# Another merge of all step chains in a two-layer kernel, with K's parts, the first stack transfers and heads 0 and 1's maxima written ahead of the second batch's FFN tail

## The reference

```
x = x + L0_ffn( L0_cond(cond, x) )          # gated FFN with quantised activations and ternary weights, inner 512
x = x + L1_ffn( L1_cond(x, cond) )
# L1_cond: 16-head causal attention (head size 8) with one extra "image" key and value per batch
# L1_ffn:  16-head full attention, layer norm, 8 experts chosen by a two-level router, layer norm
```

## Time and profile before

| | |
|---|---|
| median of 3 runs | 344.09 us (341.87 to 345.22) |
| profiled execution | 342.62 us, its span 340.5 us |
| PE busy | 286.8 us (84%) |
| DVE busy | 252.2 us (74%) |
| ACT busy | 178.2 us (52%) |
| POOL busy | 54.7 us (16%) |
| chain that ended last | PE 54%, DVE 22%, issue 16%, ACT 5%, DMA 1% |

### The profile page before, as it was taken

The page is one execution under the profiler, slowest core; times in us unless marked ns, Lnnn a source line. Parts: engine busy times, 40 slices in busy tenths (PEclk is TensorE's granted clock), DMA queues, the critical chain, the costliest instruction groups (busy, mean ns, idle before and its releaser), DMA issues.

```text
span 340.5 us, 5253 instructions
## 1 busy us (share of the span) xinstructions
PE 286.8 (84%) x1760; PEld 140.5 (41%) x1760; DVE 252.2 (74%) x754; ACT 178.2 (52%) x262; POOL 54.7 (16%) x121
## 2 busy tenths in 40 slices
PE   0363754888899999889899999999999999999992
PEld 0241432243343443433333332334344447777671
DVE  6978660999988769999999898888742133758646
ACT  2755449007575776475378866755668831221120
POOL 3069300001342332233300000002000000101001
PEclk9999995569999999999999999999999999999998
DMA  6893324711535004660014450070000000000101
GB/s 179 197 189 72 58 69 140 170 30 50 167 71 121 1 4 135 146 134 2 3 42 139 95 141 0 4 247 0 2 2 2 0 1 2 1 2 0 33 0 31
DMA packets 14990, 22.82 MB, mean 67 GB/s; under 512 B 2222, under 2 KB 12338, under 8 KB 14196
## 3 DMA queue, kind: packets, MB, share of 16 engines
q1 hardware_dynamic: 14676, 22.21, 25.4%
q0 software_dynamic: 288, 0.28, 0.6%
HBM read 13.99 MB, written 4.72 MB: 55 GB/s over the span
## 4 chain that ended last, share of the span: by engine, by line
PE 54%; DVE 22%; issue 16%; ACT 5%; DMA 1%; POOLq 0%; POOL 0%; SPq 0%; DVEq 0%; ACTq 0%
PE ps_pv L1391 13%; PE ps_t L1371 10%; PE ps_s L1348 10%; DVE mx L1066 8%; PE ps_s L1466 4%; PE ps_misc L1479 4%; DVE shared L1062 3%; DVE mx L1062 1%; DMA X<-in_x 1%; ACT probs L755 1%; DVE probs L995 1%; PE ps_misc L1324 1%; PE ps_misc L1328 1%; PE ps_misc L1354 1%; PE ps_t L1281 1%
## 5 line engine op out<-in xcount | busy, mean ns | idle before, releaser
L824 ACT ACTIVATE probs<-ps_t 128x1024 f32<-128x1024 f32 (+2 forms) x128 | 105.5, 864 | 39.6 <-PE ps_t L1371 34.2
L1066 DVE TENSOR_REDUCE mx<-ps_s 128x1 f32<-128x512 f32 x124 | 79.6, 686 | 10.2 <-PE ps_s L1348 9.8
L1348 PE MATMUL ps_s<-Ks,Qs 128*128 128x512 bf16 (+2 forms) x230 | 73.8, 350 | 8.3 <-DVE mx L1062 3.3
L1371 PE MATMUL ps_t<-Qs,Ks 128*128 128x512 bf16 (+3 forms) x256 | 62.7, 340 | 0.6 <-DMA Qs<-nmT 0.4
L1391 PE MATMUL ps_pv<-probs,Vs 128*32 128x512 f32 (+3 forms) x512 | 56.2, 523 | 0.0
L1062 DVE CUSTOM_DVE_ANT_0 shared<-ps_s,shared 128x128 bf16<-128x128 f32 (+1 forms) x106 | 46.0, 460 | 7.5 <-PE ps_s L1348 6.4
L1348 PEld LDWEIGHTS ps_s<-Ks,Qs 128*128 128x128 bf16 x230 | 21.4, 97 | 63.9 <-DVE mx L1066 32.9
L672 POOL TENSOR_SCALAR_AFFINE_SELECT probs<-probs 128x256 f32<-128x256 f32 x64 | 26.2, 414 | 50.2 <-ACT probs L824 50.0
L1371 PEld LDWEIGHTS ps_t<-Qs,Ks 128*128 128x128 bf16 x256 | 22.6, 99 | 26.7 <-issue 9.2
L677 POOL TENSOR_TENSOR shared<-shared,halves 128x4 f32<-128x4 f32 x4 | 4.1, 1035 | 166.2 <-DVE shared L890 166.2
L1466 PE MATMUL ps_s<-Qf,Ks 128*128 128x512 f32 x64 | 30.4, 598 | 0.0
(11 more groups left out here) (266 smaller groups left out, 334.5 us busy)
## 6 DMA issues: line engine op xcount, KB each, us to landing
parts_q<-Qp SPq DMA_DIRECT2D x20, 128.0 KB, 1.9
Qs<-parts_q SPq DMA_DIRECT2D x24, 96.0 KB
Ks<-parts_k SPq DMA_DIRECT2D x24, 96.0 KB
Qs<-parts_q SPq DMA_DIRECT2D x12, 192.0 KB
Ks<-parts_k SPq DMA_DIRECT2D x12, 192.0 KB
Ks<-Qs SPq DMA_DIRECT2D x2, 1024.0 KB, 11.9
parts_k<-Kp SPq DMA_DIRECT2D x12, 128.0 KB, 1.8
Qs<-Qs SPq DMA_DIRECT2D x1, 1024.0 KB, 11.8
```

Source lines behind the costliest of these rows:

```text
L824: act.activation(probs[:, half % 2, j, 0:w], ps[:, 0:w], ACT.Exp).then_inc(free[f"t{i % 2}"], 1)
L1066: last = dve.tensor_reduce(mx[:, b, t, h:h + 1], ps[:, 0:w], AX, ALU.max)
L1348: mm = pe.matmul(ps[:, 0:w], Qs[:, b, h, t * P:(t + 1) * P], Ks[:, b, h, 0:w], start=True, stop=True)
L1371: mm = pe.matmul(ps[:, col:col + w], Ks[:, b, h, kb * P:(kb + 1) * P], Qs[:, b, h, S - w:S], start=True, stop=True)
```

## The change

Only the string `MERGE` differs; every instruction is still there, with the same operands except for the PSUM bank of some scores. The first line of the table, before and after:

```
-    "ffwwTffgwffffffffffuSggff4gf44Uggg4gggggg4VS4Sv000000000000000000000400000000g0000m0i00g40000m00"
+    "fwTfffffggwfffffVffwfuggff4g4f4444Uggg4g00g00g00g00gSSSv4000000000000000000000000g0000im0000g000"
```

More of the change, by code:

```diff
@@ L50 @@
 MERGE = (
-    "ffwwTffgwffffffffffuSggff4gf44Uggg4gggggg4VS4Sv000000000000000000000400000000g0000m0i00g40000m00"
[L52 to L58, removed]
+    "fwTfffffggwfffffVffwfuggff4g4f4444Uggg4g00g00g00g00gSSSv4000000000000000000000000g0000im0000g000"
+    "0m0500g000555005AAf00E5AA00gF0AA0a00a5A00A0A0miA11Am11aaM11A1A1a1A15Ia1AA1a11A1A1a1a1MA1A1a11AA1"
+    "1a1A1A1Ia1A1aa1MA1A1im1AA1Ia1A1maA1A1a1M1aaB11IBaB11aBB11q116Bb161q11B666bBq116BGB16b1BB1111BNB1"
+    "11b1im22m222b2bbJ62B2B2B2Nb2b2B2B22B2B2b22bBJB22b2B2B22B2B2b22BB2b22NB2BmJb22Bmb22b2N2bb2C2Jb22C"
+    "b2C2r22CC22r72727cC272rC722C7c22c2CCH722c2OCC22c2KmC3Ccm33c3C3C33C3c33c3OCC33c3C33C3C3Kc33CC3c3C"
+    "3C3c33c3C3O3C3C3Kc73mC3c3m3C3CO3c33c3c3D3D3KcD33c3DD33n3D3D3n3DDQ33dddQdDP33n3DDl33d3D3Ld33Dn3DD"
+    "dmmQQexdndPDDeQDLznDDdDddxDDyDDddDPDeLDdzDxdDDyPdxddedyeLdzssxRzyxeRyesyzxszRexRyezsysxzeRxzxyeo"
+    "zyxzxxezyzxzoeyexyzzopeyepypy"
 )
```

## The result

| | before | changed |
|---|---|---|
| median, 20 executions of each on one chip | 343.72 us (341.87 to 346.49) | 342.28 us (338.30 to 345.09) |
| ratio of the executions counted, 95% interval | | 0.9914 [0.9885, 0.9943] |
| second set (change again, below) | 344.14 us | 341.79 us, 0.9937 [0.9906, 0.9968] |
| profiled execution, span | 342.62, 340.5 us | 341.17, 339.1 us |

The medians are over all executions, but the ratios leave out those over 1.5% above the fastest of their kernel: 7 of the 20 of the changed kernel here, 1 of 10 in the second set, 4 of 12, 1 of 6 and 3 of 7 in the first three experiments, and none anywhere else. By the ratios the changed kernel takes 0.6 to 0.9% less time, 2 to 3 us. Over all executions the gain is smaller: the means are 343.83 and 342.18 us here, 343.77 and 341.86 us in the second set.

What follows compares the result with a forecast made beforehand. It took the first 60 us as a ramp, with DVE, then DVE and PE in turn, then PE limiting afterwards. 1.9 + 0.2 = 2.1 us off 342.62 gave 340.5, or 342.0 on the median's scale; range 338.5 to 345.5.

Steps and rivals of the forecast that it cites:

- the sum: Whole kernel: 1.9 us at the ninth maximum plus 0.2 later, 2.1 off the profiled 342.62, giving 340.5.
- Batch 0 up to `x1`: First ramp stage: ACT starts the tail 0.7 us early, `prepare` inside it costs 2.7, `x1` at 38.7, 2.0 late.
- Q's and K's parts: Behind batch 0's `x1`: Q's first part at 44.5, K's last at 50.0, 1.8 and 4.9 us early.
- SP: Transfer issue: K's last copy at 50.5, 1.75 us landing, K stacks at 52.4, 4.2 early; scores from 56.5.
- The tail with heads 0 and 1 inside: Batch 1's FFN tail: PE holds it until 56.5, last products end at 61.5, `x1` from 61.6 to 62.65.
- The mark: Ninth maximum, after batch 1's `x1` and heads 0 and 1: predicted at 62.7 against 64.54, 1.9 us early.
- The rival that they run serially: Heads 0 and 1 in batch 1's tail: PE and DVE never overlap, 10.6 us, total 347.6; chance 0.1.
- the one that the mark comes at 60.3: Batch 1's tail: scores fit its gaps, ACT stays the pace, ninth maximum 4.2 us early, total 339.4; chance 0.2.
- The image wait: First `max` of instance 0 waits 0.55 us for the image product; 0.2 of it saved, bounds 0 and 0.55.
- The later merge "at nothing": From `q` of instance 2 on: scores, attends and values interleaved in nearly the same ratio, costed at nothing.
- The rival that it gives the gain back: Instance 3, four `values` clustered ahead of score 54: up to 2.1 us lost, total 344.1; chance 0.23.
- The clock: PE's full clock returns later after thin work at 50 to 57 us: up to 0.7 us per us; chance 0.07.

Runs made afterwards that it cites:

- second set: The unaltered changed kernel timed again beside kernels with only part of the change, against the kernel before: 341.79 us, 0.9937.
- change again: The unaltered changed kernel, timed and profiled a second time against the kernel before: 341.79 us, 0.9937.
- the first three experiments: Against before: changed order only through the first eight scores, 0.9983; only after them, 0.9887; whole, but those scores behind batch 1's `x1`, 0.9881.
- scores later: Changed order with `prepare` ahead of batch 0's tail and scores 0 to 7 one tail piece later, against before: 337.08 us, 0.9808.
- the two parts: Changed order only from score 8 to instance 2's first score, 0.9988; only from there to the end, 0.9997; both against before.
- the front alone: Changed order up to instance 0's send and first eight scores, then the order before, against before: 344.85 us, 0.9983.
- the last four experiments: Changed order with `prepare` ahead of batch 0's tail: alone 0.9828, maxima behind 0.9872, batch 1's first `ffn_up` behind `x1` 0.9869, scores one piece later 0.9808.
- the first four experiments: Against before: change only through the first eight scores 0.9983, only after 0.9887, maxima behind batch 1's `x1` 0.9881, `prepare` ahead of batch 0's tail 0.9808.
- the maxima behind the tail alone: Changed order with the eight scores of heads 0 and 1 behind batch 1's `x1` again, against before: 341.08 us, 0.9881.
- K's parts alone: Order before with only K's parts, batch 1's last `ffn_up` and the stack issue ahead of batch 1's tail, against before: 342.87 us, 0.9978.
- `prepare` early and the maxima inside: Changed order, `prepare` ahead of batch 0's tail: alone 0.9808 and 0.9828, batch 1's first `ffn_up` behind `x1` 0.9869, scores one piece later 0.9808, against before.
- the rest alone: Order before up to score 7 of instance 0 with the send, then the changed order, against before: 340.92 us, 0.9887.
- the causal part: Changed order only from behind score 7 and the send to instance 2's first score, against before: 343.22 us, 0.9988.
- the later part: Order before up to instance 2's first score, then the changed order, against before: 343.41 us, 0.9997.

## Why the prediction was right or wrong

The predicted 342.0 and the measured 342.28 agree, and the profiled execution (341.17) is 0.7 over the sum's 340.5. The average over all executions moved a little less, by 1.6 to 1.9 us where 2.1 were forecast. Not every step behind the number held.

- **Batch 0 up to `x1`: right, in another split.** First product 20.55 (20.6), `x1` 39.01 (38.7). The lead of 0.7 us at ACT's start was none (31.15 against 31.16): the small operations ended at 28.31, not 27.1, since two of them took 0.55 and 0.85 us instead of 0.16 and 0.26. Behind them DVE took batch 1's first product later, and so the copies on ACT that wait for its bank were later too. `prepare` cost 2.3, not 2.7.
- **Q's and K's parts: right.** 44.79 (44.5) and 49.93 (50.0).
- **SP: mis-sized.** The K stacks were issued at 53.86, 1.5 us later than predicted. K's last part was issued at 50.5 as predicted, but the sum took 1.75 us from issue to landing out of the earlier trace rows, and here the three took 2.2, 2.7 and 3.3 us (shown above); 50.5 + 3.3 is the 53.8. Why they landed later is open. The stacks themselves needed 3.54 us, inside the bound of 4.0. The prediction's lower estimate, 2 us behind the last K issue, is nearer: the issues end at 53.86 + 1.10 = 54.96, 2.4 us ahead of the first score. (The path that it names is GpSimd's; these transfers are issued by SP.) The first score came at 57.40 (56.5).
- **The tail with heads 0 and 1 inside: right in kind, mis-sized in the other direction.** From the first score to the last products' end 4.46 us (5.0). The mark is 1.34 us early, not 1.9. DVE's idle time is not gone, as the prediction's signs had it, but moved: it has nothing to do for 6.91 us ahead of the first maximum, and `x1` is 2.0 us later than before. The rival that they run serially fell (8 us wanted), and so did the one that the mark comes at 60.3.
- **The image wait: wrong in this execution.** I took 0.2 us off for it; it grew from 0.55 to 0.83 with PE still at half pace. In the two profiles of the changed causal order with an earlier return it is 0.24 (the change again) and nothing (scores later), as forecast or better.
- **The later merge "at nothing": the step that failed.** By the profiles, at like pace it gains 1.3 us in the causal stage, 0.3 or more in instance 1 and 0.5 to 0.8 from o_rows 1 to 3. The rival that it gives the gain back has the wrong sign: the cluster of four `values` stands in the stretch that got shorter. I had compared the orders by their ratio of scores to attends and by one cluster. That can't see 1% of a stage in which PE is busy nearly all the time. In the timed runs this gain does not stand clear of noise (0.9988 and 0.9997 for the two parts), so its size rests on the profiles.
- **The ramp as the whole gain: not borne out.** The sum counts nothing but the front, yet the front alone measured 0.9983 where the sum says 0.994. Three of its twelve executions have a mean clock of 0.969 to 0.972; of those, the profiled one has Q and K of batch 0 at half pace. The prediction had no such case: moving `prepare` into the tail costs more than its 2.3 us in some executions.
- **The clock: the rival was real, though not from the cause I gave.** I gave 0.07 to a later return. It came some 4 us later (near 79 us instead of 75) and cost 1.4 us, 0.35 for each us where the prediction allowed up to 0.7. My reason was thin work at 50 to 57 us; but the kernel with the changed causal stage and before's front has the late return too (0.50 through 77 to 80). What in the order decides it is open.

So the number came out by luck: in this pair of profiles the late return of the clock (1.4) and the dip (0.9) covered a gain in the later merge (2.4) that I had not seen, beside a lead at the mark that was 0.6 short. The prediction's sign for a failure of the later stages, a lead that changes by over 1 us between the instances, was too coarse to show it: the lead is 1.34 us at the mark and 1.22, 0.70 and 1.44 at the three `o_rows`. The profiles' 1.45 us are 1.34 + 1.3 + 0.4 + 0.7 - 1.4 - 0.9. The timed 2 to 3 us lie higher; executions with and without the dip and the late return are mixed there in both kernels.

## What to carry to other kernels

When an order is changed everywhere, cut both profiles at events that every order passes, and compare the stages one by one; two stages with opposite signs look like no change in the total. A step without a hurry (here `prepare`) does harm inside a chain that has one, and its own cost is easy to read off: moved out, it gave back 1.6 us at once and the best kernels of the study (0.981, 337.1 us). A critical transfer issued earlier is worth what the later of its partners leaves: K's parts 4.4 us early gained 0.3.

## What the runs showed of the hardware

**PE at half pace under a full recorded clock.** In three executions the fp32 products of Q and K take 2.04 and 2.08 us, exactly the length that L1324 has elsewhere while the granted clock is at 0.50 (1.98 to 2.05), but the page records full clock up to 66 us (PEclk above). In one it shows full clock up to 144 us, with the second Q at 2.05 us as well. So a mean granted clock near 1 is no proof of full pace; the length of a known matmul is. The Trainium skill, page "TensorE: Matmul & The Clock Gate", Part 1, says that idleness closes the gate and that how a kernel falls against it varies from run to run. The lengths agree with the second: the same products take 1.10 us in one profile of the change and 2.04 us in the other. That idleness lowered the pace here no run shows, and the recorded clock of these executions does not show the lower pace at all.

**One order, two levels.** 17 executions of the kernel before, timed beside the last four experiments, fall into two groups: 342.0 to 343.4 at a mean clock of 0.960 to 0.966, and 344.1 to 346.4 at 0.947 to 0.950. In the set of 17 of the first four experiments the two groups are there again; among the 27 of the second set two executions (344.47 and 344.76 us at 0.963) fit neither. The 2 to 3 us between the groups are of the size of the second Q's late return. With three executions of each kernel one can take either for a change.

**A dip near 140 us.** In 11 of the 14 profiles the granted clock falls once between 132 and 150 us (0.72 over 138 to 144 us in the changed kernel), in a stretch where PE is busy 67.55 of 72 us. PE is not without pauses there: in the changed kernel it waits 0.41 and 0.45 us in the 4 us ahead of the fall at 140 us, and with the maxima behind the tail alone it is idle from 145 to 146 us, ahead of a fall at 146 us. But the kernel before has a wait of 0.80 us at 140.8 us and no fall, so what decides is open. The dip goes with 1 to 2 us more in instance 1's stage, and the three profiles without it (before, the change again, K's parts alone) show that it is not tied to one order.

**Stack landings vary.** The time from K's stack issue to the first score, with PE waiting for it, is 3.54 (changed), 3.80, 3.52, 3.47 and 3.58 us (the four profiles with `prepare` early and the maxima inside), 4.04, 4.45 and 4.54 (before, the causal part, the later part), but 5.57 in one execution (the rest alone), with the same transfers.

**Small DVE operations beside GpSimd (POOL).** Two operations on 128x4 values take 0.16 and 0.26 us in the profile of before and 0.55 and 0.85 in that of the change. In the change POOL is at work on a subtraction, an add and the start of a memset at the same time (25.3 to 28.8 us); in the profile of before it is at work too, but on a memset alone (28.9 to 30.9 us). The Trainium skill, page "GPSIMD Engine Reference", section 1, "Specifications", says that GpSimd shares its interfaces to SBUF with VectorE and that operations with two SBUF inputs contend there; the first of the two (L1003, q with q) is one. The second (L1004) has one such input, and it lengthened more, which the two inputs do not explain. All this is read from the timelines, not tried alone.
